# A one-core decoder layer: cross attention rows added behind the fourth mask, output products between transposes, low halves last

## The reference, cut to what matters

```
scores = coef * (x @ Wq.T) @ ctx.T ; scores -= max
thr    = top_k(scores, 54)[-1]
att    = softmax(where(scores < thr, -inf, scores))
x      = layernorm(x + (att @ ctx) @ W_o.T)
```

## Time and profile before

| | |
|---|---|
| median of three runs | 939.14 us |
| the profiled execution | 938.63 us |
| its span, first to last instruction | 936.8 us |
| granted TensorE clock, mean | 0.995 |
| TensorE busy | 910.6 us, 97% |
| VectorE, ScalarE, GpSimd busy | 588.8, 579.8, 503.0 us |

### The profile page before, as it was taken

The page is one execution under the profiler, slowest core; times in us unless marked ns, Lnnn a source line. Parts: engine busy times, 40 slices in busy tenths (PEclk is TensorE's granted clock), DMA queues, the critical chain, the costliest instruction groups (busy, mean ns, idle before and its releaser), DMA issues.

```text
span 936.8 us, 13231 instructions
## 1 busy us (share of the span) xinstructions
PE 910.6 (97%) x4440; PEld 749.9 (80%) x4440; DVE 588.8 (63%) x1059; ACT 579.8 (62%) x1150; POOL 503.0 (54%) x413
## 2 busy tenths in 40 slices
PE   9999999999999999999989999799999999999997
PEld 7788788887788877887768788698888788888885
DVE  5666966678666776667584899976697125411114
ACT  4667876688766878787875566443745535433333
POOL 4357652646626467377754568534574852354440
PEclk9999999999999999999999999899999999999999
DMA  7532230122301322113112213332333341343221
GB/s 203 157 96 63 75 101 1 51 69 74 103 1 32 88 68 76 61 57 91 46 57 90 80 35 102 88 94 75 117 112 102 114 123 34 114 125 96 93 80 45
DMA packets 46102, 76.97 MB, mean 82 GB/s; under 512 B 5584, under 2 KB 11216, under 8 KB 45776
## 3 DMA queue, kind: packets, MB, share of 16 engines
q1 hardware_dynamic: 45600, 75.68, 27.2%
q10 hardware_dynamic: 432, 0.39, 0.2%
HBM read 73.69 MB, written 2.36 MB: 81 GB/s over the span
## 4 chain that ended last, share of the span: by engine, by line
PE 30%; DVE 15%; ACT 3%; issue 3%; POOL 1%; ACTq 0%; DVEq 0%; POOLq 0%
DVE m L1586 5%; PE p L899 4%; PE p L903 4%; PE p L900 4%; DVE SX L1594 2%; DVE SCL L1594 2%; PE p L913 2%; PE p L915 2%; PE p L914 2%; PE p L865 1%; DVE SX L1597 1%; PE p L866 1%; PE p L867 1%; DVE SX L1836 1%; DVE st L1546 1%
## 5 line engine op out<-in xcount | busy, mean ns | idle before, releaser
L2013 POOL TENSOR_TENSOR V<-RAW,V 128x512 fp32r<-128x512 f32 x64 | 85.5, 1359 | 131.0 <-ACT V L1082 131.0
L1513 DVE TENSOR_SCALAR_CACHE_REDUCE JK<-p,ssc 128x512 bf16<-128x512 f32 x112 | 83.7, 747 | 112.8 <-PE p L664 112.8
L1025 ACT ACTIVATE PR<-p,nms,ssc 128x512 f32<-128x512 f32 x112 | 87.4, 780 | 59.3 <-DVE JK L1513 58.0
L2009 POOL TENSOR_TENSOR acc<-SX,acc 128x512 f32<-128x512 f32 x56 | 72.4, 1293 | 82.3 <-ACT SX L1062 51.3
L682 PE MATMUL p<-R 128*128 128x512 f32 x248 | 97.3, 392 | 0.8 <-DVE V L1506 0.8
L2013 POOL TENSOR_TENSOR C<-RAW,C 128x512 fp32r<-128x512 f32 x58 | 75.3, 1310 | 31.2 <-ACT C L1082 31.2
L1836 DVE TENSOR_TENSOR SX<-p,SX 128x512 f32<-128x512 f32 x32 | 22.0, 689 | 110.2 <-PE p L903 95.5
L1526 DVE TENSOR_TENSOR PT<-p,PT 128x512 fp32r<-128x512 f32 x128 | 87.3, 682 | 5.4 <-ACT PT L1044 5.2
L717 PEld LDWEIGHTS p<-ident,PR 128*128 128x128 f32 x512 | 62.4, 140 | 21.2 <-DVE PT L1526 6.6
L717 PE MATMUL p<-ident,PR 128*128 128x128 f32 x512 | 77.4, 274 | 1.0
L1044 ACT ACTIVATE PT<-p 128x512 fp32r<-128x512 f32 x128 | 75.8, 592 | 0.0
(11 more groups left out here) (249 smaller groups left out, 2750.2 us busy)
## 6 DMA issues: line engine op xcount, KB each, us to landing
RAW<-in_wg SPq DMA_DIRECT2D x32, 256.0 KB, 2.8
RAW<-in_wu SPq DMA_DIRECT2D x32, 256.0 KB, 2.6
RAW<-in_ctxn SPq DMA_DIRECT2D x32, 256.0 KB, 2.8
RAW<-in_wd SPq DMA_DIRECT2D x32, 256.0 KB, 2.7
RAW<-in_wq SPq DMA_DIRECT2D x19, 256.0 KB, 2.7
RAW<-in_wk SPq DMA_DIRECT2D x18, 256.0 KB, 2.7
RAW<-in_wv SPq DMA_DIRECT2D x16, 256.0 KB, 2.7
RAW<-in_wo SPq DMA_DIRECT2D x16, 256.0 KB, 5.1
```

The source lines that it names most:

```text
L1025: e.activation(PR[:, i % 2, :], P[i % 2][:, :], ACT.Exp, bias=nms[:, i % 4:i % 4 + 1], scale=ssc[:, 0:1] if HB[j][0] > 1 else SC, accum_ou ...
L1513: e.tensor_scalar(JK[:, :], P[i % 2][:, :], ssc[:, 1:2] if HB[i // 4][0] > 1 else -SC, None, ALU.mult, ALU.min, accum_out=nms[:, i % 4:i % ...
L2009: e.tensor_tensor(acc[:, r], scaled_at(4 * q + tt), acc[:, r], ALU.add).then_inc(*rows[r].up((q, 1)))
L2013: e.tensor_tensor(lo, RAW[:, slot[key], :], hi, ALU.subtract).then_inc(*c_lo.up(key))
```

## The change

It has five parts.

1. `Search.alone(n)`: gives the rest of the steps of tile n by themselves and leaves the other live tile where it is. ScalarE calls it with n = 3 ahead of `px_high(2)`, in place of `until(3)` behind it.
2. VectorE's two `cross_add` of tiles 0 and 1 go from ahead of the masks of tiles 2 and 3 to either side of the mask of tile 3 (the fourth mask): tile 0's ahead of steps 3:14 and 3:15, tile 1's behind them.
3. TensorE's order x_out(0), x_out(1), px_T(2), px_T(3) becomes x_out(0), px_T(2), x_out(1), px_T(3).
4. In `x_values` and `x_out` all matmuls that need only high halves of the moving (or stationary) intermediate come first, the ones with its low half last, and the wait for the low half goes between.
5. ScalarE converts gate and up weights 2 ahead of the second `gate_act`, no longer behind it.

```diff
+    def alone(self, n):
+        z = n % 2
+        if n in self.done:
+            return []
+        assert self.live[z][0] == n
+        out = [(n, s) for s in range(self.live[z][1], 16)]
+        self.done.add(n)
+        self.live[z] = [n + 2, 0]
+        if n + 2 > 7:
+            del self.live[z]
+        return out
...
 def x_values(n, ms, banks, q):            # TensorE
-                for x in range(4 * b + q.start // 128, 4 * b + q.stop // 128):
-                    w.wait_ge(*px_lo(x).at((x, kt // 4)))
+                tiles = range(4 * b + q.start // 128, 4 * b + q.stop // 128)
+                for x in tiles:
+                    w.wait_ge(*px_hi.at((x, kt // 4)))
                 for m, k in zip(ms, banks):
...
                     e.matmul(ps, cn(n)[:, 1, c], PX[:, 0, kt, q], start=kt == 0, stop=False)
                     e.matmul(ps, cn(n)[:, 0, c], PX[:, 0, kt, q], start=False, stop=False)
-                    e.matmul(ps, cn(n)[:, 0, c], PX[:, 1, kt, q], start=False,
+                for x in tiles:
+                    w.wait_ge(*px_lo(x).at((x, kt // 4)))
+                for m, k in zip(ms, banks):
+                    e.matmul(P[k][:, q], cn(n)[:, 0, cols(m)], PX[:, 1, kt, q], start=False,
                              stop=kt == 7).then_inc(*avxp.up((n, m)))
...
 def x_out(r, k):                          # TensorE
                     e.matmul(ps, OX[:, 0, m, c], XW[:, 0, m], start=m == 0, stop=False)
                     e.matmul(ps, OX[:, 0, m, c], XW[:, 1, m], start=False, stop=False)
+                for m in range(4):
                     w.wait_ge(*ox_lo.at((b, m, stop)))
                     t = e.matmul(ps, OX[:, 1, m, c], XW[:, 0, m], start=False, stop=m == 3)
...
-            x_out(0, 4)                   # TensorE
-            x_out(1, 5)
             for n in (2, 3):
+                x_out(n - 2, n + 2)
                 for hf in range(2):
                     px_T(n, hf, 6 + hf)
...
             search(topk.until(2))         # ScalarE
+            search(topk.alone(3))
             for hf in range(2):
                 px_high(2, hf, 6 + hf)
             conv_cn()
-            search(topk.until(3))
...
             gate_act(0, (0, 1))           # ScalarE
+            conv_gu(2)
             gate_act(1, (4, 5))
-            conv_gu(2)
             conv_gu(3)
...
             search(topk.until(0))         # VectorE
-            cross_add(0, 4)
             search(topk.run(2))
             search(topk.until(1))
+            search(topk.until(2))
+            last = topk.alone(3)
+            search(last[:-2])
+            cross_add(0, 4)
+            search(last[-2:])
             cross_add(1, 5)
-            search(topk.until(2))
-            search(topk.until(3))
```

## The result

The changed kernel takes **945.02 us**, median of five runs (944.08 to 946.71), against 939.49 for five of the kernel before on the same chip: a ratio of 1.006, 95% interval 1.0049 to 1.0071. It is slower by some 5.5 us. The forecast was 944.6. The profiled execution took 944.59 with a span of 942.8, 6.0 more than before. TensorE is busy 2.2 us longer than before and stands 3.8 us longer.

What follows compares the result with a forecast made beforehand. TensorE, busy 97% of the span, was taken as the bound. Terms -2.4 - 0.65 + 5.9 + 2.6 = +5.45 on the profiled 938.63 gave 944.1, plus 0.5 for the median: 944.6 us, whole range 941.2 to 947.3.

Steps and rivals of the forecast that it cites:

- Masks of tiles 2 and 3: From 592 to 616 us: GpSimd's low half for x_values(13) comes 2.6 us earlier, net -2.4 us.
- Part 5: At gate_up(2): TensorE's wait of 0.65 us for GpSimd goes, -0.65 us.
- Tile 6: At px_T(6): TensorE newly waits for tile 6's mask, now behind gate_mul(11), +5.9 us, bounds 3.6 and 7.7.
- The clock behind tile 6: Behind the new wait at px_T(6): TensorE's clock falls to about half, +2.6 us.
- The clock in the new waits: Before 614 us: no fall of the clock in TensorE's two new waits of about 2.15 and 2.5 us.
- rival 1: Clock also falls in one of two new waits before 614 us, losing up to 2.6 us: 947.2 us, chance 0.15.
- Part 4 at x_values(16): At x_values(16): the 0.7 us wait, set by ScalarE behind gate_up(12), stays.
- One of the stated signs of being wrong: At gate_up(2): the prediction is wrong if TensorE isn't about 3 us earlier than before.
- Rival 4: At px_T(6): mask signalled before gate_up(11) ends, so only the gains stand, 936.1 us, chance 0.09.
- rival 2: At tile 6: the clock does not fall behind the wait, 942.0 us, chance 0.10.
- rival 3: At px_T(6): the wait is at its floor of 3.6 us and the clock holds, 939.7 us, chance 0.08.

Runs made afterwards that it cites:

- e5: The kernel before with only alone(3) in place of until(3) on ScalarE and VectorE: 946.13 us, ratio 1.0068.
- e1: The changed kernel with three more search entries (run(5) for run(2)) on ScalarE and VectorE ahead of the feed-forward loop: 936.49 us, ratio 0.9962 to the kernel before.
- e3: The changed kernel, but at n = 11 GpSimd makes the low halves of tile 6's weights ahead of those of gate and up weight 13: 944.17 us.
- e6: The kernel before with part 4 only, low halves last in x_values and x_out: 938.64 us, ratio 0.9989.
- e7: The kernel before with part 5 only, gate and up weights 2 converted ahead of the second gate_act: 938.02 us, ratio 0.9985.
- e4: The changed kernel with nine matmuls of ones, read by nothing, in TensorE's wait ahead of x_values(13): 943.18 us.
- e2: The changed kernel with until(3) in place of alone(3) on both engines, so all parts but the first: 938.66 us, ratio 0.9988 to the kernel before.

## Why the prediction was right

The time came out within 0.4 us, and the way there was right where it mattered, at tile 6. That it came out so near is luck: a fall of the clock that was left out (+1.4) is balanced by a gain that was forgotten (-0.8) and by two terms at tile 6 that were taken 0.2 and 0.4 too large. Step by step, with 0.7 us taken off for the later start:

- **Masks of tiles 2 and 3.** Predicted for px_T(2) 598.15, for ScalarE's exponential 599.2, for the mask of tile 3 600.4, for x_values(13) 613.7. Measured 598.06, 599.2 (599.88), 600.36 (601.06), 613.7 (614.40). The reading that GpSimd's queue of low halves, and not TensorE, ends this stage is what made this exact: TensorE was early by 1.9 at px_T(3) (1.7 predicted) and yet stood 2.42 us behind (2.5 predicted). Three terms made GpSimd 2.7 earlier: `px_low` started 1.2 sooner; it took 2.66 instead of 3.37, as the mask of tile 3 was nearly done when it started; and the idle time ahead of wd 0 was 0.47 instead of 1.25. The later high halves cost 0.3 up to x_out(2) (0.2 predicted).
- **Part 5.** -0.65 predicted, 0.7 measured.
- **Tile 6.** 5.9 predicted, 5.71 measured, with its three terms: gate_mul(11) 1.2 behind gate_up(11)'s end (1.36 predicted) because of the exponential and the table load; 2.0 for gate_mul; the mask 2.36 (2.40 predicted, by the one row of before in which it started together with GpSimd). e5 shows that part 1 alone is the cause, e1 that only the order is, and e3 that the mask's extra 1.1 is GpSimd's.
- **The clock behind tile 6.** 2.6 predicted, 2.2 measured: TensorE ran at half clock for 4.5 us and not for 6.9.
- **The clock in the new waits: this step was wrong.** I took no fall for them because the one precedent of 1.67 us had none. It fell behind the wait of 2.42, and 1.4 of the gain went. That was rival 1, at 0.15, in part: 1.4 of its 2.6.
- **Part 4 at x_values(16): forgotten.** I wrote that the 0.7 us wait stays. The same edit that I had used at x_out(0) puts four high matmuls of 0.23 ahead of it, and it is gone here and in e6. It is worth -0.8 and offsets over half of the clock term.
- **One of the stated signs of being wrong came out.** I had asked for TensorE at gate_up(2) to be about 3 us earlier than before. It was 1.05 earlier, 1.8 with the later start taken off: the 1.4 of the clock are missing there. The sign did its work; it points at the step on the clock in the new waits, not at tile 6.

Rival 4 (tile 6 not late) is refuted by the order and by the wait itself, rival 2 by the clock of 0.50, and rival 3 by the wait of 5.7.

What made the start 0.7 us later, ahead of all that TensorE does in a new order, was not found. e5 and e7, which change nothing ahead of it either, have x_out(0)'s first low product at 595.79 and 595.22 against 594.65, so differences of that size between executions occur. The first matmul of x_values(0) lies between 580.70 (e6) and 581.87 (e5) in the ten traces.

## What to carry to other kernels

When engines walk one shared order by counts ("the next five entries"), an edit that takes entries out anywhere shifts every later one. List the order again to its end, and look for a step that falls behind an operation which itself waits for the engine that needs the step: a faster engine makes such a wait shorter but does not hide it, and its floor can be added up from the rows. And if a stage is ended by a queue of another engine, cutting TensorE's waits in it only gathers them in one place, where they may cost the clock as well (e6); the stage ends earlier only if that queue starts earlier or moves faster.

## What the runs showed of the hardware that was not expected

The length of a wait does not say by itself whether the clock falls. The wait at px_T(2) was 1.90 us in the changed kernel and in e1 to e4, at the same place of the program. In the changed kernel and in e4 the clock behind it is 1.00, with the eight transposes in 1.09 us. In e1 it fell at once:

```profile
598.14 1.97 PE L862 MATMUL p<-ident,SX 128*128 128x128 f32 x8 [1.90 <-DVE SX L1614]
```

In e2 and e3 the transposes still took 1.09, and the clock fell some 1.4 us behind the wait: its mean was 0.71 in e2 from 598.2 to 604 us, and 0.59 in e3 from 600 to 604. In e5 the clock fell behind the wait of 2.19 us (0.57 from 604 to 608) and held behind 1.66. Over the traces of all ten kernels, behind 590 us: it held behind each of three waits of 1.66 or 1.67 us, fell behind three of five of 1.90, and fell behind every one of 2.19 us or more.

A fall behind the wait of 1.90 cost 1.3 us at x_values(13) (34.25 and 34.27 us from x_values(0) in e1 and e3, against 32.95 in the changed kernel and e4), one behind 2.42 cost 1.4, and the one behind 2.9 in the kernel before 2.6 by the prediction's sum. It may also be part of the spread of the changed kernel's five runs, 944.1 to 946.7, whose two longest have the lowest mean clock, 0.993 and 0.991 against 0.994; only one of the five was profiled, so this is not shown. What decides between two equal waits was not tried.
